# Attention products of a small Perceiver block: low-precision parts on block-diagonal operands replaced by float32 on 32x32 tiles of the array

## What is computed

```
x = x + matmul(fake_quant(layernorm(x)), fake_quant(ctx))       # ctx (16, 512, 512)
x = x + attention(layernorm(x))
x = x + ffn(layernorm(x))     # 64 experts of rank 8, top 16 chosen by a router

attention(h), for every token on its own:
    q, k, v = (h @ w.T + b).reshape(B, S, 32 heads, 16)
    scores  = einsum('bshd,bstd->bsht', q, k) / 4     # 32x32 for each token: head against head
    context = einsum('bsht,bstd->bshd', softmax(scores), v)
```

## Time and profile before

| | |
|---|---|
| median of 3 runs | 202.35 us (202.15 to 202.36) |
| span of the profiled execution | 198.7 us |
| TensorE busy, matmuls | 136.4 us, 69% |
| TensorE busy, weight loads (beside the matmuls) | 88.6 us, 45% |
| VectorE busy | 152.5 us, 77% |
| ScalarE busy | 93.6 us, 47% |
| GpSimd busy | 95.1 us, 48% |
| mean granted TensorE clock | 0.887 of full speed |

### The profile page before, as it was taken

How to read it: one execution, slowest core, us unless ns; L and a number is a source line. 1 busy time by engine, 2 the same in 40 slices (tenths; PEclk the granted TensorE clock), 3 DMA queues, 4 the chain that set the end, 5 groups by cost and what they waited for, 6 DMA issues and landing times.

```text
span 198.7 us, 3999 instructions
## 1 busy us (share of the span) xinstructions
PE 136.4 (69%) x1630; PEld 88.6 (45%) x1630; DVE 152.5 (77%) x258; ACT 93.6 (47%) x117; POOL 95.1 (48%) x101
## 2 busy tenths in 40 slices
PE   0012587940904799787957998597799949589884
PEld 0002473410803654336646443393754418585543
DVE  0768579999699657799997679999844999958331
ACT  0289414875892084822693856327016734301120
POOL 2738036668870858753049698313347832201000
PEclk9999999995585579997888999969699996969999
DMA  4999999995738138000000100000010000000101
GB/s 103 422 412 404 398 406 416 372 409 208 269 157 351 76 66 358 3 0 0 3 3 0 52 2 3 0 3 0 3 56 0 0 0 3 0 3 0 54 3 53
DMA packets 7218, 25.20 MB, mean 127 GB/s; under 512 B 1184, under 2 KB 1440, under 8 KB 5280
## 3 DMA queue, kind: packets, MB, share of 16 engines
q1 hardware_dynamic: 7056, 24.94, 32.7%
q10 hardware_dynamic: 144, 0.00, 0.0%
HBM read 23.89 MB, written 1.05 MB: 126 GB/s over the span
## 4 chain that ended last, share of the span: by engine, by line
DVE 53%; PE 17%; issue 12%; POOL 9%; ACT 4%; DMA 2%; POOLq 0%; DVEq 0%; ACTq 0%
PE ps_b L1098 6%; DVE qdiag L756 5%; DVE vdiag L787 4%; DVE vdiag_lo L798 4%; DVE kT L764 4%; DVE qT L743 4%; DVE h L636 3%; POOL q_sb L358 3%; DVE stats L630 3%; DVE probs L636 2%; POOL rstd L343 2%; DMA sc_in<-in_quant_dram 2%; DVE s_max L805 2%; DVE kT_lo L768 2%; DVE vdiag L929 2%
## 5 line engine op out<-in xcount | busy, mean ns | idle before, releaser
L466 ACT ACTIVATE cu<-raw,sc_in,sc_recip 128x2048 uint8<-128x2048 f32 x15 | 30.7, 2085 | 0.8 <-DMA raw<-in_ctx_dram 0.8
L1171 PE MATMUL ps_att<-qT,vdiag 128*128 128x32 f16 x128 | 17.3, 186 | 9.7 <-DVE qT L821 9.7
L352 POOL TENSOR_SCALAR cbf<-cu 128x2048 bf16<-128x2048 uint8 x10 | 19.7, 1974 | 4.8 <-ACT cu L466 4.5
L340 POOL TENSOR_SCALAR var_eps<-mean_var 128x1 f32<-128x1 f32 x12 | 3.6, 301 | 36.0 <-DVE mean_var L632 35.8
L1152 PE MATMUL ps_att<-kT,qdiag 128*128 128x32 bf16 x128 | 10.4, 183 | 14.6 <-DVE kT_lo L768 7.6
L378 POOL TENSOR_TENSOR k_pack<-probs,k_pack 128x512 f16<-128x512 f32 x7 | 9.4, 1351 | 19.0 <-ACT k_pack L535 19.0
L1152 PEld LDWEIGHTS ps_att<-kT,qdiag 128*128 128x128 bf16 x128 | 10.1, 101 | 17.8 <-issue 17.8
L1171 PEld LDWEIGHTS ps_att<-qT,vdiag 128*128 128x128 bf16 x128 | 13.2, 103 | 10.6 <-DVE vdiag_lo L798 10.6
L1172 PE MATMUL ps_att<-qT,vdiag 128*128 128x32 f16 x128 | 17.3, 186 | 0.0
L1173 PE MATMUL ps_att<-qT,vdiag 128*128 128x32 f16 x128 | 17.3, 186 | 0.0
L1174 PE MATMUL ps_att<-qT,vdiag 128*128 128x32 f16 x128 | 17.3, 186 | 0.0
(11 more groups left out here) (141 smaller groups left out, 460.7 us busy)
## 6 DMA issues: line engine op xcount, KB each, us to landing
raw<-in_ctx_dram SPq DMA_DIRECT2D x15, 1024.0 KB, 7.0
raw<-in_ctx_dram SPq DMA_DIRECT2D x2, 512.0 KB, 11.8
wq<-in_L_attn_wq_dram SPq DMA_DIRECT2D x1, 1024.0 KB, 14.1
wk<-in_L_attn_wk_dram SPq DMA_DIRECT2D x1, 1024.0 KB, 10.8
wv<-in_L_attn_wv_dram SPq DMA_DIRECT2D x1, 1024.0 KB, 15.0
wa<-in_L_ffn_A_w_dram SPq DMA_DIRECT2D x1, 1024.0 KB, 18.6
wb<-in_L_ffn_B_w_dram SPq DMA_DIRECT2D x1, 1024.0 KB, 16.1
x_sb<-in_x_dram SPq DMA_DIRECT2D x1, 768.0 KB, 8.6
```

The costliest lines, as they stand in the source:

```text
L352: nc.gpsimd.tensor_scalar(cbf[:, n % BF_SLOTS, :, :], cu8[:, n % U8_SLOTS, :], -CENTER, 1.0, ALU.add, ALU.mult).then_inc(sem_ctx_bf_pool, 1)
L466: nc.scalar.activation(cu8[:, n % U8_SLOTS, :], raw[:, n % RAW_SLOTS, :], ACT.Identity, bias=sc_in[:, 3:4], scale=sc_recip[:, 2:3]).then_i ...
L1171: nc.tensor.matmul(ps_att[:, i, :], v_hi, e_hi, start=True, stop=False)
```

## The change

`scores` and `context` run in float32 on 32x32 tiles of the array. Each token has its own matmul: batch `j` of the tile uses partitions `32j` to `32j + 31` of the operands and of the output. All the work that makes parts and block diagonals is gone, with its tensors, its clears and its semaphores. `qT`, `kT`, `eT` and `vT` are float32 tensors of their own. `q_sb` and `k_sb` get 16 padding columns, so that one transpose with overlapping 32-column windows spreads each of them over the heads (`spread_heads`, 128x1024 elements each). Line 826's transpose of the context takes 17 columns for each token, not 32. The order of the remaining work on each engine stays. The counts in `keep_clock_up` and the cut of the context at token 24 stay too.

```
-                for i in range(Q):
-                    q_hm = view(qdiag[:, :], 2 * P * i, [[2, P]])
-                    q_lh = view(qdiag[:, :], 2 * P * i + 1, [[2, P]])
-                    nc.tensor.matmul(ps_att[:, i, :], q_hm, view(kT[:, :], 2 * H * i, [[2, H]]), start=True, stop=False)
-                    nc.tensor.matmul(ps_att[:, i, :], q_hm, view(kT[:, :], 2 * H * i + 1, [[2, H]]), ...)
-                    last = nc.tensor.matmul(..., q_lh, view(kT_lo[:, :], H * i, [[1, 2], [2, H // 2]]), ...)
+                for i in range(Q):
+                    for j in range(BPT):
+                        rows = slice(Q * j, Q * j + HD)
+                        last = nc.tensor.matmul(ps_att[Q * j:Q * j + H, i, :], qT[rows, i, :], kT[rows, i, :],
+                                                start=True, stop=True)
...
-                    nc.tensor.matmul(ps_att[:, i, :], v_hi, e_hi, start=True, stop=False)
-                    nc.tensor.matmul(ps_att[:, i, :], v_hi, e_lo, start=False, stop=False)
-                    nc.tensor.matmul(ps_att[:, i, :], v_mid, e_hi, start=False, stop=False)
-                    nc.tensor.matmul(ps_att[:, i, :], v_mid, e_lo, start=False, stop=False)
-                    last = nc.tensor.matmul(ps_att[:, i, :], vdiag_lo[:, P * i:P * (i + 1)], e_hi, ...)
+                    for j in range(BPT):
+                        rows = slice(Q * j, Q * (j + 1))
+                        last = nc.tensor.matmul(ps_att[rows, i, 0:HD + 1], eT[rows, i, :], vT[rows, i, :],
+                                                start=True, stop=True)
...
-            def transpose_q, place_q, spread_k, transpose_v, place_v, spread_v_lo
+            def spread_heads(dst, src, biased, done, t):
...
+                nc.vector.transpose(dst[:, :, :].rearrange("p i h -> p h i"),
+                                    view(src[:, :], 0, [[HD, H], [1, Q]])).then_inc(done, 1)
+            def transpose_v(t):
...
+                nc.vector.transpose(vT[:, :, 0:HD].rearrange("p i d -> p d i"),
+                                    v_sb[:, :].rearrange("p (h d) -> p d h", d=HD)).then_inc(sem_vT_ready, 1)
...
 VectorE, per tile:
-                    transpose_q(t)
-                    place_q(t)
+                    spread_heads(qT, q_sb, sem_q_biased, sem_qT_ready, t)
+                    spread_heads(kT, k_sb, sem_k_biased, sem_kT_ready, t)
                     bias_v(t)
-                    spread_k(t)
...
-                    place_v(t)
...
-                    spread_v_lo(t)
...
 ScalarE: hi_q, mid_q, hi_k, hi_k_again, mid_k, hi_v, mid_v and the scaling and rounding after the softmax's exp removed
 GpSimd: take_hi, make_lo, make_e_lo removed
-            nc.gpsimd.memset(words(qdiag), 0).then_inc(sem_q_zeros, 1)
+            for padded in (q_sb, k_sb):
+                nc.gpsimd.memset(padded[:, D:], 0.0).then_inc(sem_q_pad, 1)
+            nc.gpsimd.memset(vT[:, :, HD:HD + 1], 1.0).then_inc(sem_v_ones, 1)
...
-            nc.gpsimd.memset(words(vdiag_lo), 0).then_inc(sem_v_lo_zeros, 1)
...
-            nc.vector.memset(words(vdiag), 0).then_inc(sem_v_zeros, 1)
```

More of the change, by code:

```diff
@@ L34 @@
 CUT = 24
-E_SCALE = 16384.0
 SCALING = 2.0
@@ L213, in build @@
         h2T = sb("h2T", [P, KC, P])
[L215 to L228, removed]
+        q_sb, k_sb = (sb(n, [P, D + HD]) for n in ("q_sb", "k_sb"))
+        v_sb = sb("v_sb", [P, D])
+        qT, kT, eT = (sb(n, [P, Q, H]) for n in ("qT", "kT", "eT"))
+        vT = sb("vT", [P, Q, HD + 1])
         s_max = sb("s_max", [P, Q])
         probs = sb("probs", [P, Q, H])
-        e_pack = k_pack[:, :].bitcast(F16)
-        eT = qT[:, :].bitcast(F16)
-        oT = probs
+        oT = sb("oT", [P, HD + 1, H])
         o_recip = sb("o_recip", [P, H])
-        vT = words(k_sb)
-        attn = k_sb
+        attn = sb("attn", [P, D])
         h3 = sb("h3", [P, D])
@@ L401, in _ @@
             for t in range(TILES + 1):
[L402 to L405, removed]
                 if t == TILES:
@@ L737, in transpose_q @@
+            def transpose_v(t):
+                if t == 0:
+                    dve.wait_ge(sem_v_ones, 1)
                 if t >= 1:
                     dve.wait_ge(sem_context_done, t)
[L739 to L745 removed]
@@ L747, in place_q @@
-            def place_q(t):
-                dve.wait_ge(sem_qT_ready, 2 * (t + 1))
-                if t == 0:
-                    dve.wait_ge(sem_q_zeros, 1)
-                if t >= 1:
-                    dve.wait_ge(sem_scores_done, 2 * t)
-                for j in range(BPT):
-                    rows = slice(Q * j, Q * j + Q)
-                    nc.vector.tensor_copy(
-                        words(qdiag).rearrange("p (i m) -> p i m", m=P)[rows, :, Q * j:Q * j + Q],
-                        words(qT).rearrange("p (i h) -> p i h", h=H)[rows]).then_inc(sem_q_diag, 1)
@@ L791, in spread_v_lo @@
-            def spread_v_lo(t):
-                if t == 0:
-                    dve.wait_ge(sem_v_lo_zeros, 1)
-                dve.wait_ge(sem_v_lo, t + 1)
-                for j in range(BPT):
-                    rows = slice(Q * j, Q * j + Q)
-                    nc.vector.transpose(
-                        words(vdiag_lo).rearrange("p (i m) -> p m i", m=P // 2)[rows, Q * j // 2:(Q * j + HD) // 2, :],
-                        words(v_lo).rearrange("p (h d) -> p d h", d=HD // 2)[rows]).then_inc(sem_v_diag, 1)
+                dve.wait_ge(sem_v_biased, t + 1)
@@ L928, in _ @@
             copy_q1T(0)
-            nc.vector.memset(words(vdiag), 0).then_inc(sem_v_zeros, 1)
-            dve.wait_ge(sem_v_zeros, 1)
-            for j in range(BPT):
-                nc.vector.memset(view(vdiag[Q * j:Q * j + Q, :], 2 * (Q * j + HD), [[2 * P, Q]]), 1.0)\
-                    .then_inc(sem_v_ones, 1)
             center_ctx(2)
```

215 lines of the change are left out of this document (34 added, 181 removed).

## The result

| | before | after |
|---|---|---|
| median of the runs beside each other | 202.25 us (199.48 to 202.36, 4 runs) | 190.99 us (189.19 to 192.84, 4 runs) |
| profiled execution: time, span | see the section on the profile before | 192.84 us, span 191.0 us |

The ratio after to before is 0.947, with a 95% interval of 0.937 to 0.956. The prediction was 237 us with a range of 191 to 262 and 29% for faster. The median lies at the range's lower edge, 0.01 us outside it; what came out otherwise is the direction, and with it the price of a matmul. The profiled execution was the slowest of the four, so its parts are up to 2% long.

The account below looks back on a forecast made before the run. VectorE was taken to set the pace before, TensorE to bound after. Stages and end gave a span of 130.8 + 2.048 s; at s = 50 ns, 233.2 us span, 236.9 us time, said as 237, range 191 to 262.

Parts of the forecast that it names:

- the price s: Scores and context: time between starts of float32 matmul instructions on 32x32 tiles, taken as 50 ns; one ns worth 2 us.
- Neighbouring tiles overlap: Scores and context: batches on other rows and columns run at once, s under 25, to 13 ns; rather 165 us; 5%.
- the floor of 25 ns held for every stream of the trace: Small 16-bit matmuls of 32 columns never start closer than 25 ns at full clock; argument against tiles running at once.
- The chosen 50: Scores and context: each of a float32 instruction's two passes pays the 25 ns floor, so 50 ns; 42% for the forecast.
- the first rival: Scores and context: floor paid once an instruction, passes stream, s 27 to 32 ns; 190 to 200 us, likely 195; 24%.
- the third rival: Scores and context: loads not hidden on a tile, or half clock; s 54 to 75 ns, 245 to 288 us; 17%.
- The sum: TensorE's path over all stages and the end: span 130.8 + 2.048 s us, time 134.5 + 2.048 s.
- So TensorE doesn't wait: Stages 1 and 2: VectorE's 22 us fit under TensorE's path of 23.1 us plus scores and context.
- The start: Before stage 0's scores: without the clears 3.7 us gained, first projections near 25.7 us, first scores near 40.
- The time outside the span: Whole kernel: median of the runs taken as 3.65 us above the span, kept from before.
- Stage 3's terms: Stage 3 of TensorE's path: 15.3 us, last chunk 0.9 and `keep_clock_up` 3.9, together 20.2 plus scores and context.
- The first paragraph: Kernel before: VectorE sets the pace in every stage, with TensorE only about 5 us behind.

Follow-up runs that it names:

- with half the instructions: Kernel after with scores and context reading only the upper 16 bits as bf16, one matmul instruction for a token and batch instead of two: 163.2 us, ratio 0.813.
- the halves: Kernel after with each scores product cut in two around other work, and stage 3's 18 idle matmuls split nine and nine: 180.59 us, ratio of medians 0.897.
- copies put back: Kernel after with VectorE again making four 32x1024 block copies behind q's spread, into a buffer nobody reads: 196.02 us, ratio 0.967.
- the kernel before with less for VectorE: Kernel before without the transposes of the low part of v into `vdiag_lo`: 194.92 us, ratio 0.960.
- the first experiment: Kernel after with the same matmuls reordered so that 16 (or 8) tokens of one batch follow one another on one 32x32 tile: 231.02 us, ratio 1.149.
- the fastest one: Kernel after with products in halves, the 18 idle matmuls kept, and five idle float32 matmuls before the transpose of h2 in stages 1 and 2: 176.04 us, ratio 0.869.

## Why the prediction was wrong

**The step that failed is the price s.** "Neighbouring tiles overlap" was the last rival, with 5%, and it is what happens. It was set aside because "the floor of 25 ns held for every stream of the trace". Every stream of that trace used the whole array, so it could say nothing about tiles. The three orders show it, at full clock: one tile 29 ns, two tiles 14.7, four tiles 8.6. "TensorEngine Tiling (Array Packing)" of the Trainium skill ("Tiles operate independently", under "Key Properties") agrees with that. The chosen 50 and its reason (the extra 5 ns "looks like a cost paid once a pass") do not hold even on one tile. There the first rival's 27 to 32 holds, as long as the clock is full; at half clock one tile costs 42 to 48, as the third rival feared. That the time, 191, falls into the first rival's 190 to 200 is luck: the price that it rests on isn't paid in this kernel, and other losses fill the gap.

**The sum gave a second error of the other sign.** With s = 8.6 it would be 130.8 + 17.6 = 148.4 us of span, and the rival's own 165 allowed for waits; the span was 191.0. The difference has four parts.
- Pauses for instructions. The eight products take, pauses in and waits for VectorE out, 7.35 and 7.8 us in stage 0 (whose scores start 12 ns apart, mostly at half clock), 5.3 and 3.0, 4.8 and 3.0, 5.4 and 5.5: 42.2 us, on average 21 ns an instruction. 130.8 + 42.2 = 173.0. No step and no rival had a limit of the supply. "Runtime: NRT & Kernel Launch" of the Trainium skill ("Instruction fetch mechanics") says that instructions come in blocks of 16 KiB, and that this cost is mostly hidden. The packets agree with the block; under streams of short matmuls the cost is not hidden here, 2.3 to 3.9 us for each scores product.
- Half clock behind them. The projections of q in stages 1 to 3 take 5.58, 5.31 and 4.79 us where the sum has 3.68, the projections back 4.50, 4.86 and 5.75 for some 3.7, the 18 matmuls 5.38 for 4.18, and the last chunk of the bottleneck in stage 3 2.08 for 1.12: about 10.8 us, 4.6 + 4.0 + 1.2 + 1.0. For the projections back it is the pauses: with half the instructions, where no product pauses, they take 3.68, 3.68 and 3.70 us, and in the halves, where the pauses are short, the same. The projections of q stay slow in both (5.40 to 6.48 us); before that of stage 2 it was the wait for h that had to be filled.
- Waits for VectorE. "So TensorE doesn't wait" fell: 1.21 us for the second half of the probabilities in each of stages 1 and 2, and 1.97 and 0.36 for h. Most of it is VectorE's order: the second transpose of the probabilities and the normalisation stand behind the residual, which waits for `transpose_y1`. The rest is one long operation: the normalisation before the 1.97 us took 2.15 us, the same in stage 2 took 0.55. Beside the long one, from 95.04 to 98.96, GpSimd casts a context matrix, as it cleared `qdiag` beside the long one in the earlier trace rows. The four waits are 4.8 us.

```profile
95.06 2.15 DVE L481 TENSOR_SCALAR h<-x_sb,mean_var,rstd 128x512 f32<-128x512 f32 x1 [0.45 <-POOL rstd L299]
```

- Stage 0 apart from its products: the first scores 0.8 us late, 4.5 us and not 4.2 between scores and context (1.46 of it a wait for the first product's result), the transpose of h2 1.05 and not 0.5. That is 1.6 us.

173.0 + 10.8 + 4.8 + 1.6 = 190.2 of 191.0; the rest I can't assign.

**What held.** The start: the first projection at 25.49 for 25.7, the first scores at 40.57 for 39.8. VectorE 104.1 us busy for about 110, and 22.0 in stage 2 for about 22. TensorE as the bound of the later stages, where copies put back cost almost nothing. The 18 matmuls as a load on its path. The frame of the sum: with the 82.5 us measured on one tile it lacks 16 us, as it lacks 18 here, and in both much of this is half clock.

**What was mis-sized.** The time outside the span is 1.8 us in each listed run (192.84 - 191.0), not the 3.65 that came of setting one execution's span against the median of others. Stage 3's terms add up to 20.1, not 20.2, which changes nothing. The first paragraph calls TensorE 5 us behind VectorE; by the earlier trace rows the two are 0.6 us apart, both some 5 us short of the stage. That VectorE set the pace is shown by the kernel before with less for VectorE, not by these rows.

**Why it is only 5%.** Two things were worth something and one was not. The clears (3.5 to 5.7 us) and the shorter way to the first scores (4 to 5 us) make most of the gain, 10.7 of 11.3 us by the medians and 7.7 of 10.8 by the ratios. The shorter work of VectorE in stages 1 to 3, which looks like the core of the change, went into waiting, as far as the copies put back and the lengths of the stages tell: TensorE took over as the bound at nearly the same length of stage, by pauses and half clock that the new streams bring with them. With the same instructions placed otherwise, and ten more in each of two waits, the change gives 13%.

**What stays open.** Why one tile costs 29 ns at full clock, whether a load waits for its own tile or each pass has a floor, was not separated. "TensorE: Matmul & The Clock Gate" of the Trainium skill ("Part 3: Packing small matmuls") would have the load wait if the row group is the same. The prediction made over 100 ns of that, and no order comes near it; 29 is hardly more than the 26.7 that the prediction gives for the two passes of 32 columns alone, which leaves little room for a load that waits. Nor was it separated why four tiles cost 34 ns for each tile and not 29. What fills the 2.25 to 3.0 us between a packet's transfer and the next matmul no view shows. That the pauses are waits for instructions is inferred: from the packets' times, from the count at which the streams stop in two orders, and from the two kernels with fewer instructions in a row. Halves without the five matmuls have no interval, so their gain is a difference of medians, though in range the runs do not overlap with those of the kernel after (177.32 to 181.89, against 189.19 to 192.84).

## What to carry to other kernels

A price that the trace does not show at that shape needs a lower bound from the way in which the shape could be cheaper. Small matmuls cost over three times as much on one tile as spread over four (29 and 8.6 ns at full clock), so put consecutive ones on different tiles. Once they are cheap, count the instructions: some 250 to a packet of 16 KB, and a stream of 512 at 8.6 ns a matmul runs dry in every scores product here. The same stream cut in two by a group of long matmuls paused less, 1.36, 0 and 0.24 us in stages 1, 2 and 3 for 2.60, 2.31 and 2.63. When the bound moves from VectorE to TensorE, look at what the order on VectorE holds back, and fill TensorE's remaining waits, so that the projection behind them does not run at half clock.

## What the runs showed of the hardware

- Tiles of the array keep their own pace: 29 ns from start to start on one tile, 14.7 over two (29 for each), 8.6 over four (34 for each), at full clock. At half clock it is 42 to 48 ns on one.
- A stream of short matmuls stops after the same instruction in two orders with different rates (219, 225, 218 and 213 of 256), and goes on 2.25 to 3.0 us after a 16 KB packet of instructions was moved, in 13 pauses of two kernels. From the start of the scores to the end of the pause it is 4.4 to 4.8 us in stages 1 to 3 of both, and the pause is what the stream leaves of that.
- The normalisation on VectorE took 2.15 us beside a cast on GpSimd (95.06, kernel after) and 0.55 without one (132.25), as it took 3.88 beside a clear.
- A busy TensorE does not keep its clock in every case. On one tile at a time the granted clock went to 0.50 within a scores product in which the engine was busy throughout (windows of the first experiment), while the group of long matmuls in front of it ran at full clock (six in 2.84 us). Behind the wait before the transpose of h2 in stage 2 the clock was 0.68 in the kernel after, and 1.00 in the fastest one, which has ten instructions on the whole array in that wait.
- An instruction of this size costs the same in bf16 (8.1 ns) as one of the two of a float32 matmul (8.6 ns) when they go over four tiles.
